# The feed-forward's first norms are moved into the attention's last three turns

## Reference

```
h = shift_token(x)                      # second half of the channels comes from the token before
q, k, v = split(h @ wqkv); q, k = l2norm(q)*qs, l2norm(k)*ks; rotary on both
o = local_attention(q, k, v)            # windows of 128, each sees itself and the one before
x = x + o @ wo
h = shift_token(x)
h = (h - mean(h)) / sqrt(var(h) + 1e-5) * g + b
a, gate = split(h @ w1 + b1)
x = x + (a * gelu(gate)) @ w2 + b2
```

## Time and profile before

| | us |
|---|---|
| median of 3 runs | 3231.86 |
| lowest and highest | 3226.63, 3234.86 |
| the profiled execution: its own time | 3224.11 |
| its span, first to last instruction | 3222.0 |
| PE busy | 2949.9 (92%) |
| DVE busy | 2207.8 (69%) |
| ACT busy | 1978.7 (61%) |
| POOL busy | 218.6 (7%) |
| mean granted clock of PE | 0.974 |

### The profile page before, as it was taken

The page is one execution under the profiler, slowest core; times in us unless marked ns, Lnnn a source line. Parts: engine busy times, 40 slices in busy tenths (PEclk is TensorE's granted clock), DMA queues, the critical chain, the costliest instruction groups (busy, mean ns, idle before and its releaser), DMA issues. The chain is left out here.

```text
span 3222.0 us, 70760 instructions
## 1 busy us (share of the span) xinstructions
PE 2949.9 (92%) x29314; PEld 1465.9 (45%) x29314; DVE 2207.8 (69%) x2752; ACT 1978.7 (61%) x2682; POOL 218.6 (7%) x325
## 2 busy tenths in 40 slices
PE   6999999999999999999999896999986887978878
PEld 3444444444444444444444563222234664656655
DVE  6888788888888888888788855000027775677756
ACT  5665655655656656556556424999975774267732
POOL 0000000000000000000000101100003323043200
PEclk8999999999999999999999898999998998999989
DMA  2000000000000000000000003111101001000000
GB/s 78 7 2 2 8 2 8 2 2 8 2 2 8 2 2 8 2 4 2 2 3 2 31 1 128 27 27 36 27 13 49 20 1 58 1 17 17 1 1 27
DMA packets 30032, 51.64 MB, mean 16 GB/s; under 512 B 6071, under 2 KB 22538, under 8 KB 28554
## 3 DMA queue, kind: packets, MB, share of 16 engines
q1 hardware_dynamic: 29706, 46.91, 4.7%
HBM read 41.04 MB, written 5.83 MB: 15 GB/s over the span
## 5 line engine op out<-in xcount | busy, mean ns | idle before, releaser
L734 ACT ACTIVATE a_probs<-PS 128x1024 f32<-128x1024 f32 x928 | 949.6, 1024 | 602.7 <-PE PS L489 599.5
L502 PE MATMUL PS<-a_probs,a_V 64*64 64x512 f32 x7424 | 980.0, 590 | 5.6 <-DVE a_heads_outT L915 4.6
L956 DVE TENSOR_TENSOR a_prob_sums<-a_prob_sums,a_probs 128x1024 f32<-128x1024 f32 x512 | 627.4, 1225 | 153.4 <-ACT a_probs L734 137.7
L953 DVE SCALAR_TENSOR_TENSOR a_prob_sums<-a_probs,a_valid,a_prob_sums 128x1024 f32<-128x1024 f32 x384 | 481.1, 1253 | 70.4 <-ACT a_probs L734 60.3
L489 PE MATMUL PS<-a_Q_hi,a_K_hi 64*64 64x512 f16 x3712 | 385.0, 381 | 5.5 <-ACT a_probs L734 4.7
L1772 ACT ACTIVATE c_probs<-PS 128x1024 f32<-128x1024 f32 (+1 forms) x416 | 382.9, 1080 | 8.4 <-PE PS L1691 6.6
L489 PE MATMUL PS<-a_Q_lo,a_K_hi 64*64 64x512 f16 x3712 | 384.0, 377 | 1.2 <-issue 1.1
L489 PE MATMUL PS<-a_Q_hi,a_K_lo 64*64 64x512 f16 x3712 | 382.1, 377 | 1.8 <-issue 1.8
L502 PEld LDWEIGHTS PS<-a_probs,a_V 64*64 64x64 f32 x7424 | 290.1, 133 | 165.6 <-issue 21.1
L489 PEld LDWEIGHTS PS<-a_Q_hi,a_K_hi 64*64 64x64 f16 x3712 | 119.0, 106 | 275.7 <-issue 270.4
L489 PEld LDWEIGHTS PS<-a_Q_hi,a_K_lo 64*64 64x64 f16 x3712 | 119.5, 107 | 228.0 <-issue 224.3
(11 more groups left out here) (325 smaller groups left out, 4177.6 us busy)
## 6 DMA issues: line engine op xcount, KB each, us to landing
c_Qop<-q_part SPq DMA_DIRECT2D x96, 64.0 KB, 2.2
c_Kop<-k_part SPq DMA_DIRECT2D x96, 50.0 KB, 2.0
d_raw<-in_l1f_w_dram SPq DMA_DIRECT2D x18, 256.0 KB, 3.2
d_tables<-in_rotary_dram SPq DMA_DIRECT2D x2, 2048.0 KB, 10.8
X<-in_x_dram SPq DMA_DIRECT2D x2, 1024.0 KB, 9.5
out_dram<-X SPq DMA_DIRECT2D x4, 512.0 KB, 3.5
c_cT<-in_ctxT_dram SPq DMA_DIRECT2D x1, 1601.0 KB, 6.6
a_probs<-in_ctx_dram SPq DMA_DIRECT2D x3, 512.0 KB, 5.0
```

Of the source, the lines that this page charges most:

```text
L502: last = nc.tensor.matmul(m.PS[64 * h:64 * h + 64, PVB + g, :], V[e][rows, s, 64 * h:64 * h + 64], probs[n % 4][rows, h * BANK:(h + 1) * B ...
L734: nc.scalar.activation(probs[n % 4][:], m.PS[:, b0:b0 + 2, :].rearrange("p b c -> p (b c)"), ACT.Exp).then_inc(exped, 1)
L953: nc.vector.scalar_tensor_tensor(out=sums, in0=new, scalar=valid[:, s:s + 1], in1=sums, op0=ALU.mult, op1=ALU.add).then_inc(summed, 1)
L956: nc.vector.tensor_tensor(sums, sums, new, ALU.add).then_inc(summed, 1)
```

## The change

The functions of the feed-forward's norm become methods of a class, ShiftedNorm, whose buffers now live as long as the local transformer. The instructions of the norm are the same. For the first chunks their place is another: the shift, move and copy of chunks 0 and 1 stand in turn 13 of the attention, statistics and root of chunk 0 in turn 14, stage, turn_h and move_h of chunk 0 and statistics of chunk 1 in turn 15, and split_h(0) after the last turn. The banks are other ones: SHIFT_BANKS (0, 1, 6, 6) for (6, 5, 6, 6), and H_BANKS (0, 6, 6, 6) for 6 throughout; chunk 0 so uses the banks of queries and keys, and its shift_half waits until all 16 windows are united (L2182 done). After the root in turn 14 the Exp table is loaded explicitly.

```diff
@@ windowed_attention, PE, in turn w @@
                         mix(w - 1)
+                    if w == ST - 3:
+                        tn.shift_half(pe, l, 0)
+                        tn.shift_half(pe, l, 1)
+                    if w == ST - 1:
+                        tn.turn_h(pe, l, 0)
                     if inside(w + 1):
                         turn(w + 1)
@@ ACT, at the end of turn w @@
                         root(w + 3)
+                    if w == ST - 3:
+                        tn.move_shifted(act, l, 0)
+                        tn.move_shifted(act, l, 1)
+                    if w == ST - 2:
+                        tn.root(act, l, 0)
+                        nc.scalar.preload_act_table(ACT.Exp)
+                    if w == ST - 1:
+                        tn.move_h(act, l, 0)
@@ DVE, at the end of turn w, and after the last turn @@
                         split_weights(SPLIT_AT.index(w))
+                    if w == ST - 2:
+                        tn.statistics(dve, l, 0)
+                    if w == ST - 1:
+                        tn.stage(dve, l, 0)
+                        tn.statistics(dve, l, 1)
+                tn.split_h(dve, l, 0)
@@ POOL, at the end of turn w @@
                         split_input(w + 4)
+                    if w == ST - 3:
+                        tn.copy_first_half(pool, l, 0)
+                        tn.copy_first_half(pool, l, 1)
@@ class ShiftedNorm @@
+    SHIFT_BANKS, H_BANKS = (0, 1, 6, 6), (0, 6, 6, 6)
...
+    def shift_half(self, pe, l, c):
+        nc, bank = self.nc, self.m.PS[:, self.SHIFT_BANKS[c], :]
+        if c > 1:
+            self.after(pe, "h_moved", l * CH + c)
+        else:
+            pe.wait_ge(self.s["united"], (l + 1) * ST)
+            pe.wait_ge(self.s["added"], l * ST + 4 * c + 4)
...
+    def turn_h(self, pe, l, c):
+        pe.wait_ge(self.s["staged"], l * CH + c + 1)
+        if c == 0:
+            pe.wait_ge(self.s["shift_moved"], l * CH + 2)
...
@@ shifted_ffn, PE @@
-                shift_half(0)
-                shift_half(1)
-                turn_h(0)
                 raise_tiles(0, range(LEAD))
@@ ACT @@
-                move_shifted(0)
-                move_shifted(1)
-                root(0)
-                act.wait_ge(s["ffn_in"], 48 * (l + 1))
-                move_h(0)
-                root(1)
+                tn.root(act, l, 1)
@@ DVE @@
-                statistics(0)
-                stage(0)
                 dve.wait_ge(s["ffn_in"], 48 * (l + 1))
                 nc.vector.tensor_scalar(b1[:, 0, :], b1[:, 0, :], FF_SCALE, None, ALU.mult).then_inc(s["b1_scaled"], 1)
-                split_h(0)
-                statistics(1)
-                stage(1)
+                tn.stage(dve, l, 1)
```

More of the change, by code:

```diff
@@ L1882, in load_ffn, with windowed_attention @@
         sp.dma_start(dst, src).then_inc(s[f"raw{part % RAW}_in"], 16)
-def windowed_attention(nc, m, name, Z, pw, wm, w, l, s):
+def windowed_attention(nc, m, name, Z, tn, pw, wm, w, l, s):
     base = l * ST
@@ L2361, in shifted_ffn @@
+def shifted_ffn(nc, m, name, Z, tn, pw, wm, tables, after_it, l, s):
     base = l * CH
@@ L2365, in shifted_ffn @@
         b1, b2, aff = wm.b1, wm.b2, wm.aff
[L2366 to L2370, removed]
+        hT_hi, hT_lo = tn.hT_hi, tn.hT_lo
         hidden = [sb(f"hidden{i}", [P, BANK]) for i in range(2)]
@@ L2390, in _ @@
             def _(pool):
[L2391 to L2397, removed]
                 if after_it:
@@ L2400, in _ @@
                 for c in range(2, CH):
-                    copy_first_half(c)
+                    tn.copy_first_half(pool, l, c)
             @block.tensor
             def _(pe):
[L2405 to L2422, removed]
                 def raise_tiles(c, tiles):
@@ L2457, in _ @@
                     if c == 0:
-                        turn_h(1)
+                        tn.turn_h(pe, l, 1)
                     raise_tiles(c, range(GT - 2, GT))
@@ L2462, in _ @@
                     if c + 2 < CH:
-                        shift_half(c + 2)
+                        tn.shift_half(pe, l, c + 2)
                     lower(c)
                     if c + 2 < CH:
-                        turn_h(c + 2)
+                        tn.turn_h(pe, l, c + 2)
             @block.scalar
             def _(act):
[L2470 to L2489, removed]
                 def gelu(c, t):
@@ L2509, in _ @@
                     if c == 0:
-                        move_h(1)
+                        tn.move_h(act, l, 1)
                     for t in range(GT - 2, GT):
@@ L2516, in _ @@
                     if c + 2 < CH:
-                        move_shifted(c + 2)
-                        root(c + 2)
-                        move_h(c + 2)
+                        tn.move_shifted(act, l, c + 2)
+                        tn.root(act, l, c + 2)
+                        tn.move_h(act, l, c + 2)
             @block.vector
             def _(dve):
[L2523 to L2566, removed]
@@ L2610, in _ @@
                     if c + 1 < CH:
-                        split_h(c + 1)
+                        tn.split_h(dve, l, c + 1)
                     for t in range(GT - 2, GT):
@@ L2617, in _ @@
                     if c + 2 < CH:
-                        statistics(c + 2)
-                        stage(c + 2)
+                        tn.statistics(dve, l, c + 2)
+                        tn.stage(dve, l, c + 2)
                     output(c)
@@ L2632, in local_transformer @@
         wm = LayerWeights(sb)
+        tn = ShiftedNorm(nc, m, sb, Z, shift, wm, s)
         def loads(sp):
@@ L2654, in local_transformer @@
         for l, w in enumerate(layers):
-            windowed_attention(nc, m, f"d{l}", Z, pw, wm, w, l, s)
+            windowed_attention(nc, m, f"d{l}", Z, tn, pw, wm, w, l, s)
             after_it = layers[l + 1] if l + 1 < len(layers) else None
-            shifted_ffn(nc, m, f"f{l}", Z, shift, pw, wm, tables, after_it, l, s)
+            shifted_ffn(nc, m, f"f{l}", Z, tn, pw, wm, tables, after_it, l, s)
         mixed_in, stored = m.sem("d_mixed_in"), m.sem("d_stored")
```

83 lines of the change are left out of this document (81 added, 2 removed).

## The result

The change made the kernel faster: 3213.28 us median against 3227.97 us, ratio 0.9951 with a 95% interval of 0.9937 to 0.9964 (six runs each). That is 14.7 us by the medians for the forecast 14. A second measurement of the same change gave 0.9955 (0.9943 to 0.9968).

What follows compares the result with a forecast made beforehand. The prediction took PE to bound the feed-forward, so an earlier first projection matmul moves the end. Terms 10.8 + 2.2 + 0.8 = 13.8, called 14 us, gave 3218 us by the median; range 3210 to 3229.

Steps and rivals of the forecast that it cites:

- Turn 13: Attention: shifts fill PE's gap before turn(14), 2.4 GHz is kept, 1.6 us gained; net 1.4 us early at normalize(13).
- Turn 14: Attention: Sqrt load, root and Exp load add 2.76 us before move_spread(14); normalize(14) still 0.2 us early, mask 0.5.
- rival (b): Turn 14's table loads cost more than their rows, 2.6 us per layer; gain 9, 3223; chance 0.15 jointly with Rival (a).
- Turn 15: Attention: PE idles nearly 7 us for stage(0), resumes at half clock; the attention ends 5.9 us later.
- Sum for the start: First projection matmul of the feed-forward comes earlier: 5.7 us in layer 0, 5.1 us in layer 1, together 10.8 us.
- rival (d): turn_h(0), at the head of PE's queue in turn 15, holds up everything behind it; slower, 3242; chance 0.05.
- The clock term: Start of the feed-forward: less time at half clock, bounds 0 and 2.1 us per layer, middle 1.1 taken twice, 2.2 us.
- the old wait: Early feed-forward, layer 0: PE's 0.79 us wait for DVE's statistics(1) disappears, 0.8 us gained.
- POOL's split: Layer 0 feed-forward: next weights' split starts about 7 us later, slows DVE operations; cost 0, up to 2 us as bound.
- Rival (a): PE's clock still halves in turn 13 and at the feed-forward's start; gain 9, 3223; chance 0.15 jointly with rival (b).
- Rival (c): Later weight split slows layer 0's gates up to 2 us, no clock gain, stage(0) 0.7 us late; gain 5, 3227; chance 0.06.
- Rival (e): Nothing happens: the start of the feed-forward is not what sets the end; chance 0.04.

Runs made afterwards that it cites:

- filled kernel before: The kernel before, plus four unread fp32 matmuls on PE between mix(12) and turn(14) in turn 13 of each layer; 3222.47 us in a single execution.
- root(0) late: The change, with root(0) and the Exp load moved behind move_spread(14) in turn 15, before the exponentials; ratio 0.9944 to the kernel before.
- turn_h(0) late: The change, with turn_h(0) issued after apply(15) on PE and move_h(0) after move_spread(15) on ACT; 3206.30 us, ratio 0.9927 to the kernel before.
- the early copy: The change, with POOL copying the first half of chunk 2 ahead of the split of the next layer's weights; 3211.82 us in a single execution.
- the change once more: The change as it is, measured again beside the other runs; ratio 0.9955 to the kernel before.
- combined: The change with turn_h(0) late, root(0) late, the early copy, and split_h(0) placed between normalize(15) and add(15); ratio 0.9920 to the kernel before.
- two turns: The change with only its turn 13 and 14 parts; the rest back at the start of the feed-forward's block; ratio 0.9959 to the kernel before.
- the three with a filled entry: Unread matmuls before the first projection matmul: the entry filled (0.9955), combined with more PE gaps filled (0.9881), the kernel before with all gaps filled (0.9960).
- the entry filled: The change, plus three unread fp32 matmuls on PE after mix(15), before the first projection matmul; ratio 0.9955 to the kernel before.

## Why the prediction was right, and where its terms were off

**The total: right, in part by luck.** The forecast gain was 14 us, the measured one 14.7. The forecast time, 3218 us, was 4.7 us too high, of which 3.9 us are the base: the kernel before stood at 3231.86 us by three executions and at 3227.97 by six. The terms of the sum were off in both directions, as follows.

**Turn 13: right.** 1.44 us gained at normalize(13) in layer 1 for the 1.4 forecast; layer 0 gave 1.86 (14.33 to 12.47). The cause is shown by the filled kernel before. It was the least obvious step: the gain does not come from work that is saved but from the clock.

**Turn 14: right in kind.** Two loads of 1.28 us, the next instruction 0.01 us behind each. The page's 2.66 us for a switch (the Trainium skill, ScalarE: Activation LUTs, What ACT_TABLE_LOAD costs) is not seen in these rows, and rival (b) falls with it. The run with root(0) late prices the step at 0.9 us for the mask. normalize(14) was 0.5 us early for 0.2 forecast, mask(15) 0.9 early for 0.5.

**Turn 15: right in kind, a little dear.** stage(0) ended 38.85 us after mix(12) in layer 1, forecast 39.4. The gap was 6.78 us, forecast nearly 7. From there to the first projection matmul it took 12.9 us for the forecast 13.5: turn_probs(15) took 2.60 us (3.00 in layer 0) where the forecast had 2.8 to 3.4, and with it everything came sooner. add(15) ended 4.6 us later than before on this scale (44.86 to 49.43); the forecast had 5.9 us. Sum for the start: 5.7 + 5.1 forecast, 7.03 + 6.30 measured. That the price is real is shown by the run with turn_h(0) late; rival (d) never came near, since nothing stood between invert(15) and stage(0).

**After the start: the terms of 2.2 and 0.8 us were wrong.** Measured: 0.1 us together (-0.34 and 0.44). The clock term was a middle between bounds, 1.1 us per layer, and the low bound was nearer: after 2.79 us without work PE kept the clock for the first two to four matmuls in the profiled execution, then lost it for some 3.4 us, 1.7 us lost for 2.1 before. The bounds came from gaps of 1.90 and near 5 us, and the trace of before has a closer one: ahead of the last outputs of each layer's feed-forward PE is idle for 2.08 us. In layer 0 the clock held behind it, in layer 1 it fell:

```profile
3201.22 0.27 PE L77 MATMUL PS<-d_w_hi,f_hidden_lo 128*128 128x256 f16 x1 [2.08 <-issue]
...
3201.72 0.42 PE L78 MATMUL PS<-d_w_lo,f_hidden_hi 128*128 128x256 f16 x1
```

The Trainium skill (TensorE: Matmul & The Clock Gate, HAM oscillation) tells of a kernel whose waits for data, of 3 to 5 us, throw the array back to the low clock at every step. At the 2.79 us here that happened in 7 of 10 starts, not in all.

The 0.8 us for the old wait was really gained, but POOL's split, which I had costed at 0 with a bound of 2, took 1.17 us. The step that failed is that I asked only what the split does to DVE's speed, not what is queued behind it on POOL; the early copy brings that down to 0.30 us. The two terms also hang together, which the sum left out. Where the clock held at the start of layer 0, PE waited 2.47 us for POOL's copy: holding it saves 1.7 us there, and 1.3 us of that goes back into the wait.

So the sum, 13.8 us, fits the 13.4 us of the traces by luck: a start underrated by 2.5 us stands against 2.9 us that did not come. Rival (a) was half right at the start of the feed-forward and wrong in turn 13. Rival (c)'s mechanism, POOL's later split, appeared with 1.17 us of its 2; its gain of about 5 us follows from its parts only if "no clock gain" takes in turn 13 (13.8 less 2, 2.2, 2.8 and 1.4), otherwise they leave 8. Rival (e) is refuted by every run in which the segment moved and the time moved with it.

**What lies behind the start, and what stays open.** From the first projection matmul of layer 1 to the end, the twelve traces fall into three groups, by whether the clock fell at the start and whether it fell after the idle 2.08 us ahead of the last outputs. Both, in both kernels, the change once more, turn_h(0) late and the copy early: 116.5 to 117.0 us. One of the two, in root(0) late, turn 13 filled, combined and two turns: 114.6 to 114.8. Neither, in the three with a filled entry: 113.2 to 113.5. Each fall costs about 1.7 us. The same piece of layer 0, from the first projection matmul to mix(12) of layer 1, took between 333.0 and 337.2 us. It is shortest, 333.0 to 333.3, in the three versions with the copy early, and takes 336.7 and 337.1 in the two that have the wait of 2.47 us. Open is what decides whether the clock falls after a given gap: executions whose code there is the same differ. So differences of 2 to 3 us between versions are not read as causes unless a row shows them.

## What to carry to other kernels

When work is moved forward past another stage, the in-order queue decides: put the waiting instruction behind everything that is already due, not in front of it. That took 9 us more off the time with two lines moved. Before moving anything, ask what the idle gap costs by itself: here work that nobody reads, put into PE's gaps, was worth 10 us by the medians alone and another 12 us on top of the combined version (8 us by the traces). And when a block's start moves, look at each queue whose work is tied to that start for what stands behind it.

## What the hardware showed that I had not expected

A gap of only 2.79 us between matmuls lost the clock in 7 of 10 starts of the feed-forward (the change twice over, turn_h(0) late, root(0) late, the copy early; two layers each), mostly after the work had resumed: the first rows were still 0.38 us, those 0.4 to 1.3 us later 0.63 us. In the other three, both of root(0) late among them, it did not fall. The same gaps can go either way: after 1.90 and 1.29 us of idling the second half of turn_probs(15) took 1.09 us in both layers of the kernel before, and 1.97 us in layer 1 of the same kernel with turn 13 filled. Nor is 2.08 us safe: after the idle time of that length ahead of the last outputs of the feed-forward the clock fell in 8 of 24 cases, twelve traces of two layers each. And time saved in one place can open a gap elsewhere: with the entry filled, PE's wait for POOL's copy 33 us later grew from 1.17 to 2.47 us, and the clock fell there.
